# A graph layer on one core: gathered rows added by VectorE quad by quad from three banks, in place of TensorE from one

## What is computed

```python
h = jnp.maximum(_layernorm(x, axis=-1), 0.0)
e = jnp.concatenate([h[src], h[dst]], axis=1)
m = jax.nn.relu(e @ W1 + b1) @ W2 + b2
s = jax.ops.segment_sum(m, dst, num_segments=n_nodes)
cnt = jax.ops.segment_sum(jnp.ones((m.shape[0],)), dst, num_segments=n_nodes)
x = x + s / jnp.maximum(cnt, 1.0)[:, None]
```

## Time and profile before

| | us |
|---|---|
| median of three runs | 2825.12 (2822.13 to 2827.91) |
| the profiled execution | 2839.25 |
| its span | 2837.4 |
| granted share of TensorE's full clock | 0.749 |

### The profile page before, as it was taken

How to read it: one execution, slowest core, us unless ns; L and a number is a source line. 1 busy time by engine, 2 the same in 40 slices (tenths; PEclk the granted TensorE clock), 3 DMA queues, 4 the chain that set the end, 5 groups by cost and what they waited for, 6 DMA issues and landing times.

```text
span 2837.4 us, 26976 instructions
## 1 busy us (share of the span) xinstructions
PE 1548.3 (55%) x8249; PEld 1183.2 (42%) x8250; DVE 1428.9 (50%) x3051; ACT 1189.8 (42%) x2414; POOL 1372.7 (48%) x1460
## 2 busy tenths in 40 slices
PE   1656565566465564455544555455455545555556
PEld 0545353444344443344433444344344434434444
DVE  3554343343324665456655666456565556655421
ACT  1223343444314544345444454344344444444444
POOL 6345545445555445444554435545544554554553
PEclk6878777788787777677776777767776777776778
DMA  4532222222134656556565566556565665665541
GB/s 90 163 109 60 59 61 59 60 59 58 58 98 144 202 181 189 167 169 200 179 192 154 178 188 200 186 159 183 184 192 168 186 191 174 183 186 157 174 119 43
DMA packets 258990, 408.46 MB, mean 144 GB/s; under 512 B 45128, under 2 KB 118749, under 8 KB 258841
## 3 DMA queue, kind: packets, MB, share of 16 engines
q1 hardware_dynamic: 211845, 312.84, 35.7%
q0 software_dynamic: 46432, 93.61, 12.5%
q10 hardware_dynamic: 564, 0.23, 0.0%
HBM read 388.12 MB, written 18.38 MB: 143 GB/s over the span
## 4 chain that ended last, share of the span: by engine, by line
PE 48%; issue 36%; another core or an unknown queue 9%; DVE 6%; ACT 1%; DMA 0%; DVEq 0%; SPq 0%; ACTq 0%
PE z L1374 16%; PE bank L1401 12%; PE z L1386 10%; DVE g L1153 4%; PE bank L1419 2%; PE bank L1408 2%; PE z L1445 2%; PE bank L1430 1%; PE z L1461 1%; DVE rows_b L936 1%; PE bank L1268 1%; DVE norms L920 1%; PE z L1268 1%; ACT g L812 0%
## 5 line engine op out<-in xcount | busy, mean ns | idle before, releaser
L672 POOL DMA_INDIRECT g<-p_table,src_e x1403 | 1326.1, 945 | 1425.3 <-PE bank L1401 960.5
L1153 DVE SCALAR_TENSOR_TENSOR g<-z,norms,g 128x1024 bf16<-128x1024 f32 (+1 forms) x884 | 1019.1, 1214 | 43.5 <-issue 25.3
L812 ACT ACTIVATE g<-z 128x1024 f32<-128x1024 f32 x182 | 185.6, 1020 | 1468.0 <-remote 1153.5
L1100 DVE TENSOR_TENSOR acc<-acc,bank 65x128 f32 x191 | 54.2, 284 | 1201.0 <-remote 1069.7
L1374 PE MATMUL z<-work 128*128 128x128 f32 x1464 | 258.8, 348 | 514.2 <-issue 482.9
L1374 PE MATMUL z<-w,work 128*128 128x128 f32 x1438 | 251.9, 345 | 484.3 <-issue 443.8
L1374 PEld LDWEIGHTS z<-work 128*128 128x128 f32 x1464 | 240.3, 256 | 546.0 <-issue 541.7
L1374 PEld LDWEIGHTS z<-w,work 128*128 128x128 f32 x1438 | 234.4, 253 | 512.3 <-issue 509.3
L1401 PE MATMUL bank<-work,g 128*128 128x128 f32 x2902 | 423.4, 307 | 15.4 <-issue 15.1
L1401 PEld LDWEIGHTS bank<-work,g 128*128 128x128 f32 x2902 | 414.1, 227 | 16.8 <-issue 16.7
L1386 PE MATMUL z<-g,ident 128*128 128x512 f32 x726 | 350.8, 605 | 5.8 <-issue 5.7
(11 more groups left out here) (161 smaller groups left out, 1063.6 us busy)
## 6 DMA issues: line engine op xcount, KB each, us to landing
g<-tally_table SPq DMA_DIRECT2D x816, 256.0 KB
rel_q<-rel_table SPq DMA_DIRECT2D x46, 512.0 KB
rows_b<-rel_table SPq DMA_DIRECT2D x45, 512.0 KB
g<-p_table,src_e POOLq DMA_INDIRECT x1403
g<-tally_table SPq DMA_DIRECT2D x68, 128.0 KB
work<-q_table SPq DMA_DIRECT2D x96, 64.0 KB
w<-q_table SPq DMA_DIRECT2D x96, 64.0 KB
g<-p_table SPq DMA_DIRECT2D x12, 512.0 KB
```

The source lines that it names most:

```text
L672: nc.gpsimd.indirect_dma_start(out=g[:, slot(n), j * HID:(j + 1) * HID], out_offset=None, in_=p_table, in_offset=bass.IndirectOffsetOnAxis ...
L812: nc.scalar.activation(rows_of_p(m), z[:, 0:HID * chunks_in(m)], ACT.Relu).then_inc(r_done, 1)
L1153: nc.vector.scalar_tensor_tensor(product[i % BUFFERS][:, 0:w], turned[:, 0:w], minus_q[:, d:d + 1], tally_row[i % BUFFERS][:, 0:w], ALU.ma ...
```

## The change

- `add_rows` leaves TensorE. VectorE adds the gathered rows to z, quad by quad (512 columns each), and writes the sum to the ring; ScalarE's relu then works in the ring in place. z is now three single banks, used in turn by quads (`z_of`), and `spread_q` works on one quad, with start and stop on every chunk.
- The two blocks of sums (`u_bank`) are halves of one bank, and `sum_edges` of a new block waits until the block before is copied.
- TensorE's order in round m: `times_w2` of m-2, `spread_q` of the first quad of m+1, `sum_edges(m-1)`, `spread_q` of the second quad, the dense part. The last `sum_edges` stands behind the loop.
- `Q0` is 26: 183 couples, 59 dense nodes, 767 products (59 to ten rounds, from couple 52 to 176), 212 tallies in place of 236, five a round, all `low_hot` by ScalarE; ten places in place of twelve. ScalarE's masks and members start at couple 52.
- `AHEAD_LEAST` is 14 in place of 8.

The diff, cut:

```diff
-AHEAD_LEAST, AHEAD_STEP = 8, 48
+AHEAD_LEAST, AHEAD_STEP = 14, 48
-Q0 = 28
+Q0 = 26
-GROUP_SIZES = ((128, 4), (320, 2), (QT * 128, 1))
+GROUP_SIZES = ((126, 4), (320, 2), (QT * 128, 1))
-ROUND_TALLIES, TALLY_ROUND, TALLY_PLACES = 6, 3, 12
-
-VECTOR_TALLIES = (1, 4)
+ROUND_TALLIES, TALLY_ROUND, TALLY_PLACES = 5, 3, 10
-SPAN_ROUNDS = [10] * (SPANS - 1) + [6]
+SPAN_ROUNDS = [10] * (SPANS - 1) + [5]
...
-        u_bank, turn_bank = bank[2:4], bank[4]
+        u_bank, turn_bank = [bank[2][:, 2 * WIN * k:2 * WIN * (k + 1)] for k in range(2)], bank[4]
+        z_of = [bank[0], bank[1], bank[3]]
...
             def relu(m):
-                act.wait_ge(z_done, m + 1)
-                nc.scalar.activation(rows_of_p(m), z[:, 0:HID * chunks_in(m)], ACT.Relu).then_inc(r_done, 1)
+                act.wait_ge(z_done, quads_to(m + 1))
+                nc.scalar.activation(rows_of_p(m), rows_of_p(m), ACT.Relu).then_inc(r_done, 1)
...
+            def add_rows(m):
+                for n in couple(m):
+                    dve.wait_ge(zq_done, n - Q0 + 1)
+                    if 2 * m < RAW:
+                        dve.wait_ge(raw_p_done, n - Q0 + 1)
+                    elif n == couple(m)[0]:
+                        dve.wait_ge(gathered[slot(n) // 2], rows_landed(m))
+                    rows = g[:, slot(n), 0:HID * chunks_of(n)]
+                    nc.vector.tensor_tensor(rows, z_quad(n), rows, ALU.add).then_inc(z_done, 1)
...
                         for p in tallies(m):
                             high_hot_of(p)
+                        add_rows(m)
                         dense(m)
...
-            def spread_q(m):
-
+            def spread_q(n):
+
+                m, i = couple_of(n), GROUP[n]
                 pe.wait_ge(spread_done, parts_to(m + 1))
-                if m:
-                    pe.wait_ge(r_done, m)
...
+                if n - Q0 >= len(z_of):
+                    pe.wait_ge(z_done, n - Q0 + 1 - len(z_of))
...
-            def add_rows(m):
...
                 pe.wait_ge(r_done, m + 1)
-                if m < MEMBER_FROM:
-                    pe.wait_ge(m_made, m + 1)
                 k = BLOCK[m]
+                if k and (m == 0 or BLOCK[m - 1] < k):
+                    pe.wait_ge(u_copied, k)
...
-                    add_rows(m)
                     if m >= 2 and m - 2 == BLOCK_END[BLOCK[m - 2]]:
                         times_w2(BLOCK[m - 2])
+                    if m + 1 < COUPLES:
+                        spread_q(couple(m + 1)[0])
+                    if m:
+                        sum_edges(m - 1)
+                    if m + 1 < COUPLES:
+                        for n in couple(m + 1)[1:]:
+                            spread_q(n)
                     dense(m)
-                    if m + 1 < COUPLES:
-                        spread_q(m + 1)
-                    sum_edges(m)
...
+                sum_edges(COUPLES - 1)
```

More of the change, by code:

```diff
@@ L170 @@
 MEMBER_FROM = PRODUCT_ROUND
[L173 to L179, removed]
 def products_in(m):
@@ L304, in gnn_kernel @@
         low_hot = [above_ring(512 + 256 * k, 256, BF16) for k in range(TALLY_PLACES)]
-        high_hot = [above_ring(3584 + 64 * k, 64, BF16)[:, 0:125] for k in range(TALLY_PLACES)]
-        tally_stage = above_ring(4352, 256, U16)[0:125, :]
-        q_dense = above_ring(4352, 128, F32)[0:DENSE, :]
+        high_hot = [above_ring(3072 + 64 * k, 64, BF16)[:, 0:125] for k in range(TALLY_PLACES)]
+        tally_stage = above_ring(3712, 256, U16)[0:125, :]
+        q_dense = above_ring(3712, 128, F32)[0:DENSE, :]
         tally_row = [above_ring(512 * k, 512, U16) for k in range(BUFFERS)]
@@ L313, in gnn_kernel @@
         digit_i, digit, src_of_edge = (norms[:, NC * k:NC * (k + 1)] for k in range(3))
[L314 to L318, removed]
+        high_key, low_key = (norms[:, SPANS * DENSE + NC * k:SPANS * DENSE + NC * (k + 1)] for k in range(2))
+        added, by_count = (norms[:, SPANS * DENSE + DENSE * k:SPANS * DENSE + DENSE * (k + 1)] for k in range(2))
+        minus_q = norms[:, 1020:1020 + DENSE]
+        edges_d, of_node = norms[0:125, 1081:1081 + DGROUPS], norms[0:125, 1095:1095 + PER_GROUP]
+        assert 3 * NC <= SPANS * DENSE and SPANS * DENSE + 2 * NC <= 1020 and DENSE <= min(61, NC) and DGROUPS <= 14
         work = sb("work", [128, STAGES * UNIT_COLS + 512])
@@ L846, in dense @@
                         stage_tallies(i)
-                of = [p for p in tallies(m) if not on_vector(p)]
+                of = tallies(m)
                 for p in of[0:1]:
                     far_low_of(p)
-                for p, after in zip(of, of[1:] + [None]):
-                    if after:
-                        far_low_of(after)
+                for p in of:
+                    if p + 1 in of:
+                        far_low_of(p + 1)
                     low_hot_of(p)
@@ L1126, in edge_keys_of @@
                     .then_inc(edge_keys, 1)
-                nc.vector.scalar_tensor_tensor(low_key, digit, -512.0, src_of_edge, ALU.mult, ALU.add)\
+                nc.vector.scalar_tensor_tensor(low_key, digit, 512.0, src_of_edge, ALU.mult, ALU.subtract)\
                     .then_inc(edge_keys, 1)
@@ L1141, in high_hot_of @@
                 i, j = TALLIES[p]
-                if on_vector(p):
-                    nc.vector.tensor_scalar(low_hot[p % TALLY_PLACES], low_digits, low_key[:, j:j + 1], 0.0,
-                                            ALU.is_equal, ALU.add, accum_out=low_seen[:, p % TALLY_PLACES:p % TALLY_PLACES + 1])
                 nc.vector.tensor_scalar(high_hot[p % TALLY_PLACES], columns_p[:, 0:125], high_key[:, j:j + 1],
@@ L1437, in tally @@
                 pe.wait_ge(high_hot_done, p + 1)
-                if not on_vector(p):
-                    pe.wait_ge(low_hot_done, on_scalar_to(p + 1))
+                pe.wait_ge(low_hot_done, p + 1)
                 if p == TALLY_FIRST[i]:
```

44 lines of the change are left out of this document (17 added, 27 removed).

## The result

| | before | changed |
|---|---|---|
| median of four runs, us | 2823.94 (2822.13 to 2827.91) | 2908.31 (2900.80 to 2919.86) |
| profiled execution | 2839.25 | 2904.69 |
| its span | 2837.4 | 2902.9 |
| granted share of TensorE's full clock | 0.749 | 0.712 |

The changed kernel takes 1.030 times as long, with a 95% interval of 1.0262 to 1.0339. It was forecast at 2975, 150 us above the median known then (2825.12); measured are 84 us above the one of four runs.

The account below looks back on a forecast made before the run. GpSimd and TensorE were taken to take turns, TensorE's sums being held during gathers. Span 2837.4 - 56 (tallies) + 149 (product) + 58 (tail) = 2988, scaled to 2975 us; range 2430 to 3125, the forecast's own 2835 to 3125.

Parts of the forecast that it names:

- the hold: TensorE's completions seep out slowly while GpSimd issues a batch of 16 gathers; all pending ones come 22.7 us after its start.
- S1: First sum of edges in a cycle on TensorE, sixteen passes; ScalarE's chain and the next sum wait for it.
- B: Start of a GpSimd batch of sixteen gathers, from which times within a cycle are counted in us.
- Rival 2: The hold goes altogether, if identity adds or TensorE's waits on gathers cause it: 1975 us, chance 0.08.
- The sum behind the next spread: Product stretch: each sum waits for ScalarE's 5.9 us chain; cycle 33.4 us, +149 us (bounds +77 and +239).
- I take S1 out at the release: Product stretch: 24 passes at over 0.63 us end at B+21.1 or later, so S1 comes at B+22.7; chance 0.57.
- Rival 1: S1 seeps out early, by B+14: cycle 25.6 us, 2440 us in all, chance 0.22; turns at B+20.2.
- The tally stretch: Stretch before the dense product, without ScalarE's chain: 26 us a cycle, -56 us (bounds -124 and +4).
- free run: Couples that run without a batch of gathers beside them: 9.3 us each with ScalarE's chain instead of 6.7.
- The tail: After the last batch's start, longer look-ahead leaves seven couples instead of three: 84 us instead of 26.1, +58 us.
- VectorE's adds: Adds moved from TensorE to VectorE: about 0.69 us each, hidden, and priced at nothing beside the gathers.
- Rival 3: VectorE's adds lock gathers out, 0.55 us each, 187 us more: 3160 us, chance 0.05.

Follow-up runs that it names:

- e6: Changed kernel with TensorE's sum of edges put back ahead of both spreads, on the chip with the hold: 2575.60 us, 0.9114 of the kernel before.
- e1: Changed kernel with TensorE's sum of edges put back ahead of both spreads, on a chip without the hold: 1850.65 us, 1.0004 of the kernel before.
- e3: Changed kernel with ScalarE's first mask step done twice from couple 52 on, on a chip without the hold: 2154.80 us, 1.1647 of the kernel before.

## Why the prediction was right, and where its sizes were off

**The bound and the hold.** Right. In each of the 60 cycles of the product stretch VectorE's add of the second half spread, which stands behind S1 on TensorE, starts at B+22.5 to B+22.8, as ScalarE's relu did at B+22.8 before. Rival 2, that it goes with the identity adds or with TensorE's waits on gathers, fell: the couples of the changed kernel have neither, and it is there as before. The chips without it show that the kernel's code alone does not make it, which the prediction did not consider.

**The sum behind the next spread.** Right, and shown by e6: 344.9 us in the product stretch hang on this order alone. The chain measured 5.9 us, as priced. The term was mis-sized, +82.5 for +149. The step that failed is "I take S1 out at the release": of the 60 cycles of the product stretch 32 have the copy of S1 at B+17.6 to 20.5, not B+22.7, and they average 31.6 us (31.0 without one of 51.4 that holds two further couples), while the other 28 average 33.7. All 60 average 32.25 us, the two further couples left out, for the 33.4 of the forecast, and that difference is all but the whole miss of this term.

The pace itself was not too slow: during the hold TensorE moves on by one pass in about 0.70 us (e6 above), and the copies of S1 lie in steps of that size, at B+19.8, 20.5, 21.2, 21.9 and 22.6. What failed was to put all 24 passes at that pace. In the cycle shown VectorE's add of the first half spread starts at 1313.64, B+9.0, so its eight passes, issued from B+5.7 on, were out by then; the sixteen of S1 at 0.70 us are 11.2, and from about B+8.6 that gives B+19.8, an estimate that fits the copy at B+19.7. In the 16 cycles with S1 out at B+22.5 or later this add starts only at B+9.1 to B+12.1; why it varies was not found. Nor did show S1 at the release in the kernel before: they show the identity add behind it there, and that signals leave in program order puts S1 before the add, not close to it.

Rival 1's turning point lay too late: S1 out by B+20.2 was to give a cycle of 30.9 and break even. By the same terms S1 at B+19.7 gives 30.4, and the cycle took 31.4. The second part of the term, TensorE's 24 passes behind the chain, I put between 2.95 and 5.6 us, 4.2 in the forecast's 33.4; they took 5.5 (1330.30 to 1335.78), the slow end, and this is what rival 1's turning point lacked. From 1330 to 1336 the granted clock was 0.53, about the lower level of 1.2 GHz, after TensorE had stood idle from 1326 to 1330:

```profile
1326.00:1330.00 4.00, 0.00 (x0) 0.00 (x0) 2.77 (x4) 3.94 (x7) 0.00 (x0) 0.50 0.00 0
1330.00:1336.00 6.00, 5.70 (x28) 5.70 (x29) 5.94 (x12) 1.38 (x5) 0.00 (x0) 0.53 0.53 193
```

**The tally stretch.** -59.9 for -56. Of the 24 distances between starts of batches 11 are 23.0 to 24.1 us, the floor as priced, 11 are 26.5 to 29.8, and two, with free run in them, 38.2 and 46.4. That in the longer ones a sum is left over at the release, as the prediction has it, was not read from each:

```profile
399.19 0.94 POOL L668 DMA_INDIRECT g<-p_table,src_e  x1 [8.91 <-PE bank L1388]
...
422.64 0.94 POOL L668 DMA_INDIRECT g<-p_table,src_e  x1 [3.75 <-PE bank L1388]
...
452.46 0.94 POOL L668 DMA_INDIRECT g<-p_table,src_e  x1 [10.13 <-PE bank L1388]
...
475.77 0.94 POOL L668 DMA_INDIRECT g<-p_table,src_e  x1 [3.61 <-PE bank L1388]
```

**The tail.** +45.0 for +58: 71.1 us instead of 84. The gathers' part is 15.7 us for 17 (2831.76 to the copy at 2847.49). The six couples behind it take 46.1 for 56, but not evenly: copies at 2858.74, 2869.50 and 2881.29 are 11.3 us apart on average, slower than the 9.3 of free run, and the last three couples take 12.3 together, since one of them waits for the mask of a single quad and two for none. The last means take 9.3 for 11. In the one long gap between batches of the product stretch, too, copies are 10.4 us apart:

```profile
1251.46 0.27 ACT L812 COPY sums_u<-bank 128x128 f32<-128x128 f32 x1 [3.73 <-PE bank L1388]
...
1261.88 0.27 ACT L812 COPY sums_u<-bank 128x128 f32<-128x128 f32 x1 [3.56 <-PE bank L1388]
```

**VectorE's adds.** Rival 3 fell. A gather takes 948 ns against 945, an add 684 to 685 ns against the 0.69 us priced; 1411 x 3 ns is 4 us. The Trainium skill (SBUF — State Buffer, section "SBUF: two separate sides") has VectorE take the port pair that it shares with GpSimd when it reads two inputs from SBUF; by that rule an add with one operand from PSUM leaves the gathers alone, and the trace agrees: 948 ns.

**What the change was worth otherwise.** The forecast did not say it, e6 does: with the sum kept first, the rest of the change is worth 2826.92 - 2575.60 = 251 us with the hold. In e6 the awaited sum needs 5.0 us behind the release, in the kernel before 7.5, because relu and the full spread no longer stand between. Without the hold it is worth nothing (e1, 1.0004), since GpSimd's gathers are then the bound.

## What to carry to other kernels

When an instruction is moved on an engine, follow what its new predecessor waits for, around the loop, until it comes back to the instruction itself: here TensorE lost 12% of its busy time (1364.8 against 1548.3 us) and each sum gained a chain of 5.9 us on another engine. Where two engines take turns, let the waiting one ask for no more than what can be finished before its turn ends; halving the batch was worth 527 us in the kernel before and 610 in the changed one, more than any reordering. Time a kernel on more than one chip before tuning its waits: the sum's place and the smaller batches bring it 9 to 19% below the kernel before on one and half a percent at most on the others.

## What the runs showed of the hardware

The same kernel takes 2826.92 us on one chip and 1849.42 and 1848.51 on two others. The changed kernel with the sum first is 2575.60 (e6) against 1850.65 (e1) for identical code. On the slow one TensorE's work comes out late while GpSimd issues indirect gathers: the release is 1.41 to 1.44 us per gather of the batch after its start, and within the batch TensorE's records stand multiples of 0.70 us apart, half of that time. Whether the matmuls themselves end late or only their completion, the profile can't tell, since it models their ends. ScalarE and VectorE are not held: in the batch shown TensorE starts within 0.1 us of the end of ScalarE's mask (1310.12 + 0.18, then 1310.36), and their instructions last as long as elsewhere. On the chips without the hold the copy that was read in e3 follows the sum's recorded end by 0.04 us, with gathers of the same 945 to 948 ns. What distinguishes the chips was not found. Each chip was used in one group of runs, so no run here could tell a fault, a setting, the time of the run or another kind of placement apart.
